# Layer 1: the shared expert's products moved into the router's block, its result kept and added among the routed experts

## The chip, the cores and the metric

The kernel runs on one core of one Trainium2 chip. The metric is the device time of one execution in microseconds; the time shown is the median of three runs. Beside it stands one profiled execution, from which all durations are read. Its span reaches from the first instruction to the last. The engines are TensorE (PE, with its weight loads as PEld), VectorE (DVE), ScalarE (ACT), GpSimd (POOL) and SyncE (SP), which issues the DMAs here.

## The reference, cut to what matters

The program is four layers of cross-attention and feed-forward network over 2048 tokens of 256 features. The change concerns the feed-forward network of layer 1 alone, a mixture of 32 experts with one shared expert:

```python
def _moe_forward(x3, gate_w, w_gate_up, w_down, ws_gate_up, ws_down):
    ...
    logits = x @ gate_w.T
    grouped = logits.reshape(T, G, E // G)                 # G = 8 groups of 4 experts
    group_scores = jnp.max(grouped, axis=-1)
    _, group_idx = jax.lax.top_k(group_scores, TG)         # TG = 3
    ...
    probs = jax.nn.softmax(scores.astype(jnp.float32), axis=-1)
    topk_w, topk_idx = jax.lax.top_k(probs, K)             # K = 6
    ...
    pos = jnp.take_along_axis(jnp.cumsum(oh, axis=0) - 1, flat_e[:, None], axis=1)[:, 0]
    valid = pos < C                                        # C = 48 places per expert
    ...
    out = jnp.einsum('tk,tkh->th', topk_w.astype(x.dtype), y_pairs)
    gu_s = x @ ws_gate_up
    gs, us = jnp.split(gu_s, 2, axis=-1)
    out = out + jax.nn.silu(gs) * us @ ws_down
    return out.reshape(b, s, h)

x = x + _L1_ffn_ref(_layernorm(x, axis=-1), ...)
```

It is applied to 16 blocks of 128 tokens, each with its own counting of places. The last three lines of the function are the shared expert. It needs the normalised rows and its weights, nothing of the router.

## The kernel before, in words

`stage_l1_experts` (line 2120) holds the tokens in `X`, 16 tiles of 128 tokens by 256 features in SBUF. It is a sequence of blocks. Within a block each engine has its own instruction list, written out by hand, and waits on semaphores; between blocks all engines meet at a barrier, and a `Stage` clears its semaphores in a small block of its own when it closes. No planner orders anything: the order of the code is the order of each queue.

The blocks of the layer are, in order:

- `f1n` (`normalised_transposed`, line 1121): statistics, normalised rows, their transposes into `xnt` (2 x 2048 columns). The loads of the shared expert's weights (`w13_raw`, `w2`) are issued there.
- `f1g` (`router_logits`, line 1169): 32 products on TensorE, one copy of the logits on VectorE.
- `f1r`, the router's block: VectorE finds the groups (`choose`, "cg"), masks, takes the softmax (exponential on ScalarE), chooses six experts ("ch"); TensorE counts (`earlier`, `sums`, lines 2230 and 2232); VectorE turns counts into places; TensorE transposes the places (line 2236), VectorE copies them (line 2222). SyncE issues the loads of the first six pairs of routed experts.
- `f1d`, the dispatch: one-hot rows on VectorE, products on TensorE (line 2311) bring the tokens to their experts.
- `f1w`, the routed experts: 16 rounds, a pair of experts each; VectorE multiplies (line 2433) and writes results (line 2437).
- `f1c`, the combine: products back to the tokens, added to `X` (lines 2500, 2502).
- `f1e`, the shared expert (`GatedExperts.run`): for each quarter of 512 tokens and each of three tiles of 128 hidden features, a gate and an up product (line 1340), Silu on ScalarE (line 1380), the multiplication on VectorE (line 1394) and the down product (line 1358); then the result is added to `X` (line 1400). To keep precision, rows and weights are split into a high part (rounded to fp32r) and a low part (the rest), and each product is three products: high by high, high by low, low by high. GpSimd splits the weights and three quarters of the rows there, ScalarE and VectorE the first quarter.

Then the statistics of layer 2's attention begin (`a2s`, line 128).

## Time and profile before

| what | value |
|---|---|
| median of three runs | 3017.01 us (3011.09, 3017.01, 3017.39) |
| profiled execution, its own time | 3011.44 us |
| its span | 3009.7 us |
| mean granted clock of TensorE | 0.889 |
| busy: PE, PEld, DVE, ACT, POOL | 77%, 56%, 62%, 49%, 51% |
| layer 1's feed-forward network, from statistics to next statistics | 684.4 to 1039.4 us |

### The profile page before, as it was taken

The page shows a single profiled execution, that of the slowest core. Times are in us where ns is not written, and L with a number is a line of the kernel's source. Part 1 is how long each engine was busy: PE and PEld are TensorE (multiplying, and loading weights), DVE is VectorE, ACT ScalarE, POOL GpSimd, SP SyncE. Part 2 cuts the span into 40 slices and gives each one's busy share as a digit, 9 for nine tenths or more (in the row PEclk, how much of TensorE's full clock was granted, in tenths as well). Part 3 has the DMA queues.
Part 4 walks back from the last instruction along what each step waited for, and adds up shares of the span by engine and source line. Part 5 has one row for each costly group of instructions (what it writes and reads, how often), then busy time and mean ns, then how long its engine had stood idle before and what let it go on. Part 6 is the DMA issues. An engine that isn't in the chain of part 4 may idle for free. (4 is left out here: it accounts for less than half of the span.)

```text
span 3009.7 us, 46369 instructions
## 1 busy us (share of the span) xinstructions
PE 2304.6 (77%) x14574; PEld 1687.5 (56%) x14574; DVE 1877.6 (62%) x3732; ACT 1484.4 (49%) x3339; POOL 1525.3 (51%) x1499
## 2 busy tenths in 40 slices
PE   4887133873888757669738888886999996899997
PEld 2333011433545634358527776764788885788885
DVE  3776486654536225445568888875688885666565
ACT  0667252660120025524348777775777874344443
POOL 5542002620000244148347777772888883688882
PEclk9999665895999869979869999998999998899999
DMA  5242101543040033323220000001000000244343
GB/s 128 61 96 62 42 0 33 147 138 118 4 173 1 23 78 81 81 74 101 65 85 1 0 0 0 0 15 65 6 5 5 3 2 18 74 112 113 101 117 90
DMA packets 119749, 174.62 MB, mean 58 GB/s; under 512 B 25389, under 2 KB 79693, under 8 KB 116383
## 3 DMA queue, kind: packets, MB, share of 16 engines
q1 hardware_dynamic: 119583, 172.53, 20.4%
q8 instruction: 90, 1.47, 0.2%
q14 instruction: 76, 0.62, 0.1%
HBM read 122.49 MB, written 11.48 MB: 45 GB/s over the span
## 5 line engine op out<-in xcount | busy, mean ns | idle before, releaser
L478 DVE TENSOR_REDUCE a_mraw<-a_first_ps 128x4 f32<-128x1024 f32 (+1 forms) x256 | 310.7, 1222 | 146.8 <-PE a_first_ps L329 146.5
L386 ACT ACTIVATE a_et<-a_second_ps 128x1024 f32<-128x1024 f32 x256 | 262.2, 1024 | 161.6 <-PE a_second_ps L347 159.6
L2804 POOL TENSOR_SCALAR a3x_raw<-a3x_raw,a3x_mu,a3x_dev 128x128 f32<-128x128 f32 x320 | 282.4, 895 | 5.2 <-issue 5.2
L2804 POOL TENSOR_SCALAR a3o_raw<-a3o_raw,a3o_mu,a3o_dev 128x128 f32<-128x128 f32 x256 | 231.7, 916 | 4.8 <-issue 4.8
L1712 DVE TENSOR_TENSOR f3e_hidden_low<-f3e_hidden,f3e_hidden_high 128x512 fp32r<-128x512 f32 x96 | 116.0, 1209 | 126.3 <-ACT f3e_hidden_high L1670 125.9
L1581 POOL TENSOR_TENSOR f3e_product<-f3e_silu,f3e_up 128x512 f32<-128x512 f32 x96 | 143.3, 1495 | 72.0 <-PE f3e_u_ps L1597 44.9
L364 PE MATMUL a_o_ps<-a_et,a_vt 128*32 128x256 f32 x2048 | 167.4, 399 | 7.4 <-ACT a_osb L416 6.1
L347 PE MATMUL a_second_ps<-a_qs,a_ks 64*128 64x256 bf16 (+2 forms) x896 | 117.7, 298 | 64.7 <-ACT a_et L386 54.7
L329 PE MATMUL a_first_ps<-a_ks,a_qs 64*128 64x256 bf16 (+2 forms) x1280 | 122.4, 266 | 18.9 <-DMA a_ks<-a_parts 10.2
L347 PEld LDWEIGHTS a_second_ps<-a_qs,a_ks 64*128 64x128 bf16 (+1 forms) x896 | 42.0, 96 | 165.3 <-ACT a_et L386 129.2
L1706 DVE TENSOR_TENSOR f3e_hidden<-f3e_product,f3e_spread 128x512 f32<-128x512 f32 x96 | 125.1, 1304 | 6.8 <-DMA f3e_spread<-f3e_shares 6.8
L1663 ACT ACTIVATE f3e_silu<-f3e_g_ps 128x512 f32<-128x512 f32 x96 | 57.5, 599 | 144.2 <-PE f3e_g_ps L1597 137.2
L2974 ACT ACTIVATE a3x_weights<-a3x_s_ps,a3x_nmax 128x128 f32<-128x128 f32 x256 | 91.1, 377 | 59.6 <-DVE a3x_nmax L3108 59.6
L2795 POOL TENSOR_TENSOR a3o_dev<-a3o_var,a3o_minus_half 128x24 f32<-128x24 f32 x16 | 69.0, 4309 | 96.9 <-DVE a3o_var L3096 96.9
L1322 POOL CAST f_w_high<-f_w_raw 128x512 fp32r<-128x512 f32 x3 | 2.8, 942 | 219.9 <-SPq L1301 219.9
L2974 ACT ACTIVATE a3o_weights<-a3o_s_ps,a3o_nmax 128x128 f32<-128x128 f32 x256 | 93.0, 410 | 26.9 <-DVE a3o_nmax L3108 26.4
L2933 PE MATMUL a3o_o_ps<-a3o_wparts,a3o_catq 128*128 128x256 bf16 x768 | 102.5, 287 | 0.8 <-DVE a3o_catq L3128 0.7
L2852 PE MATMUL a3o_p_ps<-a_wq,a3o_xq 128*128 128x512 f32 x256 | 81.7, 446 | 27.2 <-ACT a3o_vv L2989 16.5
L2852 PE MATMUL a3x_p_ps<-a_wkv,a3x_ctx_parts 128*128 128x512 f32 x384 | 101.7, 408 | 0.0
L2795 POOL TENSOR_TENSOR a3x_dev<-a3x_var,a3x_minus_half 128x24 f32<-128x24 f32 x16 | 69.0, 4311 | 59.8 <-DVE a3x_var L3096 59.8
L329 PEld LDWEIGHTS a_first_ps<-a_ks,a_qs 64*128 64x128 bf16 (+1 forms) x1280 | 71.6, 100 | 45.5 <-issue 16.4
L2933 PE MATMUL a3x_o_ps<-a3x_wparts,a3x_catq 128*128 128x256 bf16 x768 | 94.2, 273 | 0.7 <-DVE a3x_catq L3128 0.7
(547 smaller groups left out, 6968.3 us busy)
## 6 DMA issues: line engine op xcount, KB each, us to landing
f_w<-in_f_w SPq DMA_DIRECT2D x16, 1216.0 KB, 8.5
a_qs<-a_parts SPq DMA_DIRECT2D x144, 128.0 KB, 2.4
f_raw<-in_f_w SPq DMA_DIRECT2D x60, 256.0 KB, 3.4
a_ks<-a_parts SPq DMA_DIRECT2D x96, 128.0 KB, 2.4
f3e_spread<-f3e_shares SPq DMA_DIRECT2D x64, 192.0 KB, 3.0
f2e_spread<-f2e_shares SPq DMA_DIRECT2D x36, 256.0 KB, 3.4
f3e_spread<-f3e_shares SPq DMA_DIRECT2D x64, 128.0 KB, 3.1
f_raw<-in_f_w SPq DMA_DIRECT2D x60, 128.0 KB, 3.4
```

What stands on the lines that cost most here:

```text
L329: last = nc.tensor.matmul(self.first_ps[:, g % 2, u, c * N:c * N + N], self.queries(p, self.ROWS, b, tq, rows), self.keys(p, self.ROWS, b, ...
L347: last = nc.tensor.matmul(out, self.keys(p, self.ROWS_WITH_MAXIMA, b, t, rows), self.queries(p, self.ROWS_WITH_MAXIMA, b, tq, slice(0, N)) ...
L364: last = nc.tensor.matmul(self.o_ps[32 * j:32 * j + 32, columns], self.vt[:, b // 2 % self.NV, b % 2, c, self.block(k, j), :], self.et[:, ...
L386: self.nc.scalar.activation(self.et[:, g % self.WAVES_HELD, :, :], self.second_ps[:, :, :], ACT.Exp, scale=self.scale).then_inc(self.e_rea ...
L478: v.tensor_reduce(out, self.first_ps[:, g % 2, :, :].rearrange("p u (c n) -> p u c n", n=N), AX.X, ALU.max).then_inc(self.max_taken, 1)
L1581: nc.gpsimd.tensor_tensor(product[:, n % self.PRODUCTS, :], silu[:, n % 2, :], up[:, n % 2, :], ALU.mult).then_inc(product_ready, 1)
L1706: nc.vector.tensor_tensor(hidden[:, n % 3, :], product[:, n % self.PRODUCTS, :], spread[:, n % self.SPREAD, :], ALU.mult).then_inc(hidden_ ...
L2795: nc.gpsimd.tensor_tensor(dev[:, :], var[:, :], minus_half[:, :], ALU.pow)
L2804: mm = nc.gpsimd.tensor_scalar(head, head, mu[:, h:h + 1], dev[:, h:h + 1], ALU.subtract, ALU.mult)
L2852: mm = nc.tensor.matmul(out, lhs, rhs, start=(i == 0), stop=(i == len(pairs) - 1))
L2933: mm = nc.tensor.matmul(o_ps[:, 0:D], catq[:, u % 2, h, :], wparts[:, p, 4 * u + h, :], start=(u == 0 and h == 0 and p == 0), stop=(u == U ...
L2974: mm = nc.scalar.activation(weights[:, u % 2, h, :], s_ps[:, h, :], ACT.Exp, bias=nmax[:, u % 2, h:h + 1], accum_out=total[:, u % 2, h:h + 1])
```

## The change

The shared expert's block `f1e` at the end is gone. Its work is spread over three earlier places:

- In the logits' block, ScalarE rounds all rows and weights to their high parts and VectorE subtracts to get the low parts, beside the logits' products on TensorE.
- In the router's block, TensorE has the twelve gate-and-up pairs and four quarters of the down product in its list, and the router's count and transposes stand between them at fixed places. VectorE's twelve hidden products stand between the router's steps, given by the argument `between` of `choose` and `softmax_rows`. ScalarE has the Silus around the exponential, and copies the result of each quarter to a tile `shared_y`. The intermediate tiles lie in the room of `xnt`. The counts, and the transposes after them, share two banks of PSUM, so that the transposes now come in four parts.
- In the routed experts, VectorE adds one tile of `shared_y` to `X` behind each of the 16 results.

```diff
-def router_logits(nc, xnt, gate, n_experts, logits, name):
-
...
-def choose(nc, values, k, n, chosen, st, name):
+def choose(nc, values, k, n, chosen, st, name, between=lambda place: None):
...
         v.max(top[:, b, :], values[:, b, :])
+    between("maxima")
...
+        if step == 4:
+            between("counts")
...
+    between("ranks")
...
+        between(dve)
...
-class GatedExperts:
...
+    def logits_and_parts(self, xnt, gate, n_experts, logits, name):
...
                 @block.scalar
                 def _(act):
-                    nc.scalar.copy(self.x_high[:, 0, :, :], xnt[:, :, rows(0)]).then_inc(x_high_ready, 1)
                     for tb in range(4):
-                        for t in range(L):
-                            n = tb * L + t
-                            act.wait_ge(gate_done, n + 1)
-                            wait(act, hidden_ready, n - 1)
-                            nc.scalar.activation(silu[:, n % 2, :], g_ps[:, n % 2, :], ACT.Silu).then_inc(silu_ready, 1)
+                        rows = slice(tb * 512, tb * 512 + 512)
+                        nc.scalar.copy(self.x_high[:, :, rows], xnt[:, :, rows]).then_inc(x_split, 1)
+                    act.wait_ge(self.w_in, 16 * len(self.loads))
+                    nc.scalar.copy(self.high[:, :, :, :, :], self.raw[:, :, :, :, :]).then_inc(w_high, 1)
 
                 @block.vector
                 def _(dve):
-                    dve.wait_ge(x_high_ready, 1)
-                    nc.vector.tensor_tensor(self.x_low[:, 0, :, :], xnt[:, :, rows(0)],
-                                            self.x_high[:, 0, :, :].bitcast(F32), ALU.subtract
-                                            ).then_inc(x_low_ready, 1)
                     for tb in range(4):
-                        for t in range(L):
-                            n = tb * L + t
-                            dve.wait_ge(silu_ready, n + 1)
-                            dve.wait_ge(up_done, n + 1)
-                            wait(dve, down_done, n - 1)
-                            last = nc.vector.tensor_tensor(hidden[:, n % 2, :], silu[:, n % 2, :], u_ps[:, n % 2, :],
-                                                           ALU.mult)
-                            last.then_inc(hidden_ready, 1)
-                        dve.wait_ge(down_done, tb * L + L)
-                        for k in range(4):
-                            x = X[:, tb * 4 + k, :]
-                            last = nc.vector.tensor_tensor(x, x, y_ps[:, k, 0:D], ALU.add)
-                        last.then_inc(added, 1)
+                        rows = slice(tb * 512, tb * 512 + 512)
+                        dve.wait_ge(x_split, tb + 1)
+                        nc.vector.tensor_tensor(self.x_low[:, :, rows], xnt[:, :, rows],
+                                                self.x_high[:, :, rows].bitcast(F32), ALU.subtract)
+                    dve.wait_ge(w_high, 1)
+                    nc.vector.tensor_tensor(self.low[:, :, :, :, :], self.raw[:, :, :, :, :],
+                                            self.high[:, :, :, :, :].bitcast(F32), ALU.subtract)
+                    dve.wait_ge(logits_done, 1)
+                    nc.vector.tensor_copy(logits[:, :, :], lp[:, :, :])
...
+    def pe_gate_up(self, pe, n):
+        tb, t = divmod(n, self.TILES)
+        wait(pe, self.silu_ready, n - 1)
+        self.product(self.g_ps[:, n % 2, :], t, 0, tb).then_inc(self.gate_done, 1)
+        wait(pe, self.hidden_ready, n - 1)
+        self.product(self.u_ps[:, n % 2, :], t, 1, tb).then_inc(self.up_done, 1)
+
+    def pe_down(self, pe, tb):
+        L = self.TILES
+        pe.wait_ge(self.hidden_ready, tb * L + L)
+        wait(pe, self.y_kept, tb)
+        for k in range(4):
+            for t in range(L):
+                last = self.nc.tensor.matmul(self.y_ps[:, k, :], self.hidden[:, tb % 2, t, k * P:k * P + P],
+                                             self.w2[:, t, :], start=(t == 0), stop=(t == L - 1))
+        last.then_inc(self.down_done, 1)
+
+    def act_silu(self, act, n):
+        act.wait_ge(self.gate_done, n + 1)
+        wait(act, self.hidden_ready, n - 1)
+        self.nc.scalar.activation(self.silu[:, n % 2, :], self.g_ps[:, n % 2, :], ACT.Silu).then_inc(self.silu_ready, 1)
+
+    def act_keep(self, act, tb):
+        act.wait_ge(self.down_done, tb + 1)
+        for h in range(2):
+            k = 2 * h
+            last = self.nc.scalar.copy(self.y[:, 4 * tb + k:4 * tb + k + 2, :], self.y_ps[:, k:k + 2, :])
+        last.then_inc(self.y_kept, 1)
+
+    def dve_hidden(self, dve, n):
+        tb, t = divmod(n, self.TILES)
+        dve.wait_ge(self.silu_ready, n + 1)
+        dve.wait_ge(self.up_done, n + 1)
+        wait(dve, self.down_done, tb - 1)
+        self.nc.vector.tensor_tensor(self.hidden[:, tb % 2, t, :], self.silu[:, n % 2, :], self.u_ps[:, n % 2, :],
+                                     ALU.mult).then_inc(self.hidden_ready, 1)
...
+                        for n in range(3):
+                            shared.act_silu(act, n)
+                        on_act(act)
+                        for n in range(3, 6):
+                            shared.act_silu(act, n)
+                        shared.act_keep(act, 0)
+                        shared.act_silu(act, 6)
+                        shared.act_silu(act, 7)
+                        shared.act_keep(act, 1)
+                        for n in range(8, 11):
+                            shared.act_silu(act, n)
+                        shared.act_keep(act, 2)
+                        shared.act_silu(act, 11)
+                        shared.act_keep(act, 3)
+
+                        def between_groups(place):
+                            if place == "ranks":
+                                shared.dve_hidden(dve, 0)
+
+                        def between_experts(place):
+                            shared.dve_hidden(dve, {"maxima": 3, "counts": 4, "ranks": 5}[place])
+
+                        def take_turned(k):
+                            dve.wait_ge(turned_done, k + 1)
+                            v.tensor_copy(placet[0:E, k * 512:k * 512 + 512], counts[0:E, k % 2, :]).then_inc(turned_taken, 1)
+
+                        choose(nc, group_top, KG, G, keep, rt, "cg", between_groups)
+
+                        v.tensor_tensor(grouped, grouped, keep[:, :, :].unsqueeze(3).broadcast_to([P, B, G, E // G]),
+                                        ALU.mult)
+                        shared.dve_hidden(dve, 1)
+                        v.drain()
+                        on_dve(dve)
+                        choose(nc, logits, K, E, chosen, rt, "ch", between_experts)
+                        v.tensor_copy(valid[:, :, :], chosen[:, :, :]).then_inc(chosen_ready, 1)
+
+                        shared.dve_hidden(dve, 6)
+                        dve.wait_ge(counted, 1)
...
+                        shared.dve_hidden(dve, 7)
+                        v.tensor_tensor(place1[:, :, :], src[:, :, :], earlier[:, :, :], ALU.add)
...
+                        take_turned(0)
+                        take_turned(1)
+                        shared.dve_hidden(dve, 8)
+                        take_turned(2)
+                        take_turned(3)
+                        for n in range(9, 12):
+                            shared.dve_hidden(dve, n)
+
...
+                        def turn(k):
+                            pe.wait_ge(places_ready, 1)
+                            wait(pe, turned_taken, k - 1)
+                            for b in range(4 * k, 4 * k + 4):
+                                last = nc.tensor.transpose(counts[0:E, k % 2, (b % 4) * P:(b % 4) * P + P],
+                                                           place1[:, b, :], ident[:, :])
+                            last.then_inc(turned_done, 1)
+
+                        for n in range(6):
+                            shared.pe_gate_up(pe, n)
+                        shared.pe_down(pe, 0)
+                        shared.pe_gate_up(pe, 6)
+                        count()
+                        shared.pe_gate_up(pe, 7)
+                        shared.pe_down(pe, 1)
+                        turn(0)
+                        turn(1)
+                        shared.pe_gate_up(pe, 8)
+                        turn(2)
+                        turn(3)
+                        shared.pe_gate_up(pe, 9)
+                        shared.pe_gate_up(pe, 10)
+                        shared.pe_down(pe, 2)
+                        shared.pe_gate_up(pe, 11)
+                        shared.pe_down(pe, 3)
...
                                                                ALU.mult, ALU.subtract).then_inc(y_taken, 1)
+                                x = X[:, q - 2, :]
+                                nc.vector.tensor_tensor(x, x, shared_y[:, q - 2, :], ALU.add)
...
-        experts.run(X, xnt, "f1e")
```

On TensorE in the router's block, before (names: `f1r_earlier` and `f1r_sums` are the two counts, `f1r_turned` the transposes):

```order
L1175 UNCONDITIONAL_BRANCH
L2224 UNCONDITIONAL_BRANCH [waits barrier_Pool_Activation_PE_DVE_SP_release]
L2230 MATMUL f1r_earlier<-f1r_chosen,f1r_before 128x512 [waits f1r_chosen_ready,f1r_const_in]
L2232 MATMUL f1r_sums<-f1r_chosen,f1r_ones 128x512
L2236 MATMUL f1r_turned<-f_ident,f_place 32x128 [waits f1r_places_ready]
L2236 MATMUL f1r_turned<-f_ident,f_place 32x128 x15
L2167 UNCONDITIONAL_BRANCH
```

Now, the piece of the same block around the count (`f1r_g_ps` and `f1r_u_ps` are gate and up, `f1r_y_ps` down, `f1r_counts` the counts); this is the first quarter of down, pair 6 and the count:

```order
L1336 MATMUL f1r_y_ps<-f1h_w,f1h_xnt 128x256 [waits f1r_hidden_ready]
L1336 MATMUL f1r_y_ps<-f1h_w,f1h_xnt 128x256 x11
L1319 MATMUL f1r_g_ps<-f1h_x_high,f1h_w_high 128x512 [waits f1r_silu_ready]
L1319 MATMUL f1r_g_ps<-f1h_x_high,f1h_w_high 128x512
L1319 MATMUL f1r_g_ps<-f1h_x_low,f1h_w_high 128x512 x2
L1319 MATMUL f1r_g_ps<-f1h_x_high,f1h_w_low 128x512 x2
L1319 MATMUL f1r_u_ps<-f1h_x_high,f1h_w_high 128x512 [waits f1r_hidden_ready]
L1319 MATMUL f1r_u_ps<-f1h_x_high,f1h_w_high 128x512
L1319 MATMUL f1r_u_ps<-f1h_x_low,f1h_w_high 128x512 x2
L1319 MATMUL f1r_u_ps<-f1h_x_high,f1h_w_low 128x512 x2
L2225 MATMUL f1r_counts<-f1r_chosen,f1r_before 128x512 [waits f1r_chosen_ready,f1r_const_in]
L2226 MATMUL f1r_counts<-f1r_chosen,f1r_ones 128x512
```

The count stands behind seven gate-and-up pairs and one quarter of down in TensorE's queue, where it was first in its block.

On VectorE in the router's block, before, at the end of the groups' choice (`f1r_keep` marks the groups kept):

```order
L1217 COPY f1r_cg_run<-f1r_cg_run 128x16x4
L1220 TENSOR_TENSOR f1r_keep<-f1r_cg_run,f1r_cg_count 128x128
L1222 SCALAR_TENSOR_TENSOR f1r_keep<-f1r_keep,f1r_cg_equal 128x128
L1224 TENSOR_TENSOR f1r_keep<-f1r_keep,f1r_cg_above 128x128
L2193 TENSOR_TENSOR f1r_logits<-f1r_logits,f1r_keep 128x512
L1241 TENSOR_REDUCE f1r_sm_max<-f1r_logits 128x16
L1243 TENSOR_TENSOR f1r_probs<-f1r_logits,f1r_sm_max 128x512
```

Now (the rows that write `f1h_xnt` are hidden products of the shared expert, in the room of `xnt`):

```order
L1196 COPY f1r_cg_run<-f1r_cg_run 128x16x4
L1357 TENSOR_TENSOR f1h_xnt<-f1h_xnt,f1r_u_ps 128x512 [waits f1r_up_done,f1r_silu_ready]
L1202 TENSOR_TENSOR f1r_keep<-f1r_cg_run,f1r_cg_count 128x128
L1204 SCALAR_TENSOR_TENSOR f1r_keep<-f1r_keep,f1r_cg_equal 128x128
L1206 TENSOR_TENSOR f1r_keep<-f1r_keep,f1r_cg_above 128x128
L2180 TENSOR_TENSOR f1r_logits<-f1r_logits,f1r_keep 128x512
L1357 TENSOR_TENSOR f1h_xnt<-f1h_xnt,f1r_u_ps 128x512 [waits f1r_up_done,f1r_silu_ready]
L1223 TENSOR_REDUCE f1r_sm_max<-f1r_logits 128x16
L1225 TENSOR_TENSOR f1r_probs<-f1r_logits,f1r_sm_max 128x512
L1357 TENSOR_TENSOR f1h_xnt<-f1h_xnt,f1r_u_ps 128x512 [waits f1r_up_done,f1r_silu_ready]
```

Three hidden products stand in this piece, each with a wait for a Silu and an up product, and the router's steps are queued behind them.

On TensorE behind the combine, before (line 2476 is the combine's last product, line 1340 the shared expert's):

```order
L2476 MATMUL f1c_out_ps<-f1x_results,f1c_back 128x512 x8
L2454 UNCONDITIONAL_BRANCH
L1332 UNCONDITIONAL_BRANCH
L1340 MATMUL f1e_g_ps<-f_x_high,f_w_high 128x512 x2
L1340 MATMUL f1e_g_ps<-f_x_low,f_w_high 128x512 x2
L1340 MATMUL f1e_g_ps<-f_x_high,f_w_low 128x512 x2
L1340 MATMUL f1e_u_ps<-f_x_high,f_w_high 128x512 x2
L1340 MATMUL f1e_u_ps<-f_x_low,f_w_high 128x512 x2
```

Now (line 2493 is the same last product, line 1032 belongs to layer 2's attention):

```order
L2493 MATMUL f1c_out_ps<-f1x_results,f1c_back 128x512 x8
L2471 UNCONDITIONAL_BRANCH
L1006 UNCONDITIONAL_BRANCH
L1032 MATMUL a_m_ps<-a_ident,a_xn 128x128 x4
L1040 MATMUL a_m_ps<-a_xt,a_wq 128x256 x4
L1049 MATMUL a_m_ps<-a_ctx,a_wk 64x256 x2
```

The shared expert's products no longer stand between the combine and the next layer.

## Rows read from the trace of the kernel before

**Rows 1.** Windows: stretch us, busy us (instructions) per engine, granted clock, DMA
```profile
976.20:1039.40 63.20, 55.35 (x240) 46.37 (x240) 15.90 (x31) 8.23 (x13) 16.83 (x13) 0.94 0.00 1
717.96:754.30 36.34, 6.78 (x20) 3.39 (x20) 26.13 (x83) 0.63 (x1) 1.80 (x1) 0.58 0.52 209
```

**Rows 2.** Timeline, ends of the shared expert: start, us, engine, line, work [idle<-releaser]
```profile
975.79 0.42 DVE L2502 TENSOR_TENSOR X<-X,f1c_out_ps 128x256 f32<-128x256 f32 x1
...
977.02 1.04 ACT L1374 CAST f_x_high<-f_xnt 128x1024 fp32r<-128x1024 f32 x1 [104.98 <-PEq L43]
...
1035.55 1.42 DVE L1400 TENSOR_TENSOR X<-X,f1e_y_ps 128x256 f32<-128x256 f32 x4 [2.71 <-PE f1e_y_ps L1358]
...
1039.39 5.32 DVE L128 BATCH_NORM_STATS2 a2s_stats<-X  x16 [2.43 <-SPq L43]
```

**Rows 3.** Timeline, TensorE's weight loads in the shared expert
```profile
980.12 0.50 PEld L1340 LDWEIGHTS f1e_g_ps<-f_x_high,f_w_high 128*128 128x128 f32 x2 [7.77 <-issue]
...
984.39 0.41 PEld L1340 LDWEIGHTS f1e_g_ps<-f_x_high,f_w_high 128*128 128x128 f32 x2
...
987.11 1.71 PEld L1358 LDWEIGHTS f1e_y_ps<-f_w,f1e_hidden 128*128 128x128 f32 x8
...
988.84 0.41 PEld L1340 LDWEIGHTS f1e_g_ps<-f_x_high,f_w_high 128*128 128x128 f32 x2
```

**Rows 4.** Timeline, VectorE in the router's block
```profile
718.00 0.69 DVE L2189 TENSOR_REDUCE f1r_group_top<-f1r_logits 128x128 f32<-128x512 f32 x1 [0.64 <-PEq L43]
...
722.06 0.29 DVE L1220 TENSOR_TENSOR f1r_keep<-f1r_cg_run,f1r_cg_count 128x128 f32<-128x128 f32 x1
...
737.80 0.43 DVE L2198 COPY f1r_valid<-f1r_chosen 128x512 f32<-128x512 f32 x1
...
741.86 0.09 DVE L2201 MEMSET f1r_totals<- 128x32 f32 x1 [3.63 <-PE f1r_sums L2232]
...
752.02 2.28 DVE L2222 CAST f_placet<-f1r_turned 32x2048 bf16<-32x2048 f32 x1 [3.54 <-PE f1r_turned L2236]
```

**Rows 5.** Windows over the logits' products and the shared expert's start
```profile
703.20:717.40 14.20, 13.38 (x64) 13.28 (x64) 0.69 (x1) 0.00 (x0) 0.00 (x0) 0.52 0.00 1
...
984.00:988.00 4.00, 4.00 (x20) 3.33 (x19) 1.08 (x2) 0.60 (x1) 3.18 (x2) 1.00 0.02 4
```

**Rows 6.** Groups by line: names, shapes, count | busy us, mean ns | idle
```profile
L1394 DVE TENSOR_TENSOR f1e_hidden<-f1e_silu,f1e_u_ps 128x512 f32<-128x512 f32 x12 | 8.3, 688 | 32.1 <-PE f1e_u_ps L1340 28.0 <-ACT f1e_silu L1380 4.1
...
L1380 ACT ACTIVATE f1e_silu<-f1e_g_ps 128x512 f32<-128x512 f32 x12 | 7.2, 599 | 46.1 <-PE f1e_g_ps L1340 46.1
...
L1400 DVE TENSOR_TENSOR X<-X,f1e_y_ps 128x256 f32<-128x256 f32 x16 | 5.7, 417 | 10.8 <-PE f1e_y_ps L1358 10.8
...
L1385 DVE TENSOR_TENSOR f_x_low<-f_xnt,f_x_high 128x1024 fp32r<-128x1024 f32 x1 | 2.0, 1957 | 1.9 <-ACT f_x_high L1374 1.9
```

**Rows 7.** Group by line: a fp32r subtraction of 128x1024 on VectorE
```profile
L2566 DVE TENSOR_TENSOR a_wkv<-a_wraw,a_wkv 128x1024 fp32r<-128x1024 f32 x4 | 4.9, 1224 | 4.5 <-ACT a_wkv L2558 4.5
```

**Rows 8.** Timeline, ScalarE: a copy, and a table load with its neighbours
```profile
663.86 0.58 ACT L416 COPY a_osb<-a_o_ps 128x512 f32<-128x512 f32 x1
...
1116.11 1.28 ACT L386 ACT_TABLE_LOAD   x1
1117.41 1.02 ACT L386 ACTIVATE a_et<-a_second_ps 128x1024 f32<-128x1024 f32 x1
```

**Rows 9.** Timeline, VectorE in two rounds of the routed experts
```profile
835.18 0.34 DVE L2433 TENSOR_TENSOR f1w_gated<-f1w_silu,f1w_gu_ps 128x176 f32<-128x176 f32 x1 [0.54 <-ACT f1w_silu L2416]
...
837.73 0.34 DVE L2433 TENSOR_TENSOR f1w_gated<-f1w_silu,f1w_gu_ps 128x176 f32<-128x176 f32 x1 [0.54 <-ACT f1w_silu L2416]
```

**Rows 10.** Timeline, TensorE in the first rounds of the dispatch
```profile
760.61 5.14 PE L2311 MATMUL f1d_x_ps<-f1d_hot,f1d_parts 128*128 128x512 f32 x12 [8.70 <-DVE f1d_parts L2290]
...
766.46 3.03 PE L2311 MATMUL f1d_x_ps<-f1d_hot,f1d_parts 128*128 128x512 f32 x12
```

325 lines of the change are left out of this document (123 added, 202 removed).

## The prediction, made before the changed kernel ran

> **What bounds the kernel now.** I read the windows by stage first. The shared expert of layer 1 stands alone at the end of that layer: from 976.2 to 1039.4 TensorE is busy 55.35 of 63.20 us at a granted clock of 0.94, and VectorE only 15.90 [rows 1]. The router's block, 717.96 to 754.30, is the mirror image: VectorE 26.13 of 36.34 us, TensorE 6.78, granted clock 0.58 [rows 1]. So one stretch is bound by TensorE, the other by a chain of small VectorE steps, and nothing of the first needs anything of the second: both read only the transposed rows. The timeline shows how far the shared expert is exposed: VectorE ends the routed part at 975.79 + 0.42 = 976.21 and starts the next layer's statistics at 1039.39 [rows 2]. Everything between is on the path.
>
> **Term 1, what goes: -61.2 us.** Of the 63.18 us between 976.21 and 1039.39, two stage boundaries (drain, semaphore clears, new block) take 977.02 - 976.21 = 0.81 and 1039.39 - (1035.55 + 1.42) = 2.42 [rows 2]. Afterwards there is one. It cannot cost less than the smaller nor more than the larger; I take 2.0, nearer the second, because the layer's stage still closes there, less the clears of the shared expert. 63.2 - 2.0 = 61.2, with bounds 60.8 and 62.4.
>
> **Term 2, the router's block grows: +24.4 us.** I price TensorE's new programme from starts of its weight loads in the shared expert. The first gate-and-up pair (12 products of 512 columns) takes 984.39 - 980.12 = 4.27 us from cold, the next 987.11 - 984.39 = 2.72, eight passes of the down product 988.84 - 987.11 = 1.73 [rows 3]. A quarter of the down product is 24 passes, 5.19. The counting products held VectorE 3.63 us and the transposes 3.54 at the low level [rows 4]: half is 1.7 each. Sum: 4.27 + 11 x 2.72 + 4 x 5.19 + 1.7 + 1.7 = 58.4.
>
> Then the waits, by a schedule from the block's start, t = 0 at 718.00 [rows 4]. Each hidden product adds 0.69 to VectorE, each Silu takes 0.60 on ScalarE [rows 6]. TensorE's pairs end at 4.3, 7.0, 9.7, 12.4, 15.2 and 17.9, the first quarter of down at 23.1, pair 6 at 25.8; then comes the count. VectorE reaches the place of the first hidden product at 722.06 - 718.00 = 4.06 and waits about half a microsecond for the up product's end and the semaphore; the second and third wait as little. Before, it had the experts chosen at 737.80 + 0.43 - 718.00 = 20.2 [rows 4]; with six hidden products and 1.4 of waits it is 20.2 + 4.1 + 1.4 = 25.7. So both come to the count at about the same time, and TensorE is the later by nothing to speak of. The count ends at 27.5. From there the places took 752.02 - 3.54 - 741.86 = 6.6 [rows 4]; with one more hidden product VectorE has them near 35.0, while TensorE, with pair 7 and the second quarter of down, comes to the transposes at 35.4. Neither wait decides, by 0.1 and 0.4 us. From there VectorE only follows. In total it has 36.3 less its two waits, 29.1, plus 12 x 0.69 = 37.4 of 58.4. One wait of TensorE remains: after the last up product it has nothing in front of the last down, and stands for 0.69 and two semaphore steps, 0.9. Behind the last product ScalarE keeps two 128x512 tiles, 0.58 each [rows 8], and the step to it is 0.2: 1.4. Total 58.4 + 0.9 + 1.4 = 60.7, against 754.30 - 718.00 = 36.3 before: +24.4. If TensorE were warm from the start it would be 1.6 less (4.27 against 2.72).
>
> ScalarE changes its table three times in the block. A load takes 1.28 us: it starts at 1116.11, right behind the copy ahead of it, and the operation behind it at 1117.41 [rows 8]. The first hides before the first gate product, the third behind the exponential. The second stands between the third Silu, done near 9.3, and the exponential, which ends near 11.2; VectorE is done with the third hidden product at 10.7 and waits about as long as it waited for the exponential before. So nothing is added. The Trainium skill (ScalarE: Activation LUTs, What ACT_TABLE_LOAD costs) adds a drain of about 1.38 us to every switch. The trace disagrees: no such gap stands on either side of that load. With the page's figure the exponential and the count come 1.4 us later and the sum is about 1.3 higher.
>
> **Term 3, parts beside the logits: 0.** In the logits block ScalarE now rounds the rows (four of 1.04) and the weights (128x1536), VectorE subtracts. VectorE's 128x1024 subtraction is 1.96 us where GpSimd works beside it [rows 6], and 1.22 for the same shape elsewhere [rows 7]. GpSimd is idle here. With the rounding of the first rows at 1.04 [rows 2], VectorE is done even by the dear end at 703.2 + 1.1 + 4 x 1.96 + 1.5 x 1.96 = 715.1; the logits come at 716.7, after 13.38 us of products [rows 5]. By the cheap end it is done by 711. Cover 1.6 us or more; if it went, each microsecond would count. The loads of these weights were issued there before as well.
>
> **Term 4, the adds among the routed experts: +0.35 us.** Sixteen adds of 128x256 go behind the sixteen result steps on VectorE. The nearest row is the add of the same shape with one operand in PSUM, 0.42 [rows 6]. In a round VectorE stands idle 0.54 us right there, waiting for the next Silu [rows 9], so the add fits with 0.1 to 0.2 to spare. Only the last one, behind the last result, is exposed: 0.35. Bounds: 0 and 16 x 0.42 = 6.7, if the gap were not where the row has it. I take 0.35 since gap and add are both rows.
>
> **Term 5, closing the block: +0.4.** Nine more semaphores are cleared in the two stages (seven and two). The larger boundary costs 1.61 more than the smaller for 18 more of them, at most 0.09 each; I take half, since it closes a stage more; bounds 0 and 0.8 [rows 2].
>
> **What stays.** Before, TensorE starts the dispatch from cold: 12 products in 5.14 us, later 3.03 [rows 10]. Now it works until 1.4 us before the block's end, but the wait for the places and the first rows stays about 6 us, so it stands some 7.5; and 7.77 us of idleness before the shared expert, which came out of a busy stretch, ended in a cold start [rows 3]. I book nothing; bounds -2.1 and 0.
>
> Sum: -61.2 + 24.4 + 0 + 0.35 + 0.4 = -36.0. The profiled execution spans 3009.7 us and took 3011.4; so span 2973.7 and time 2975.4. The median of the three timed runs is 5.6 above the profiled one (3011.1, 3017.0, 3017.4 in all), so taken from the median it is 2981. I forecast 2979, between the two and nearer the median.
>
> **Rivals.**
> A, the clock stays at 1.2 GHz in the router's block; this is my rival on the slower side. For it: the logits kept TensorE busy 13.38 of 14.20 us and the granted clock stood at 0.52 [rows 5], so being busy is not enough there. Against it: these same products of 512 columns were granted 1.00 from 984 on [rows 5], 4 us after starting, in the same ping-pong with ScalarE and VectorE. The work of 58.4 - 1.6 = 56.8 at the high level doubles at the low one to 113.6, the block becomes 115.9 with its wait and tail, +79.6, and the span 3009.7 - 61.2 + 79.6 + 0.75 = 3028.9: time 3031, slower by 0.6%. Each microsecond of that work done at the low level costs one more; the gain is used up when some 37 of the 56.8 run low, and it is measurably slower from 43. Hence a part of A (a clock that swings, a quarter of the work low) gives 2975.4 + 14 = 2990. The Trainium skill (TensorE: Matmul & The Clock Gate, A second HAM failure mode: psum-queue depth-cycling) says that short idle gaps between groups of products that cycle through PSUM banks can make the clock swing between its levels. By that rule with half the work low the time would be 3004. The shared expert cycles through two banks for each of its outputs and shows 1.00, so the trace disagrees so far.
>
> B, the two programmes do not mesh: VectorE comes late to the count and to the places, TensorE stands, and each stall shifts everything behind it. For it: margins of 0.1 and 0.4 us, and twelve fixed places for hidden products. Against it: VectorE's work is 37 of 61 us, and a lag of 1 us at either place costs 1. I allow 1 to 5 in all: time 2976 to 2980, with the median's offset 2982 to 2986.
>
> C, the adds are on the path in the routed experts: up to 6.7, time 2982, with the median's offset 2987. For it: a gap with 0.1 us to spare. Against it: a round there is 837.73 - 835.18 = 2.55 us [rows 9].
>
> D, the change doesn't do what it says: some barrier or shared tile puts the expert behind the router again, the block is 36.3 + 60 and the time as before. Against it: TensorE's order has seven pairs ahead of the count, and they wait for nothing of the router.
>
> **How the numbers follow.** Forecast with its own range 2972 to 2987: 0.83. B beyond 2 us 0.07, C 0.04, A in part (swinging) 0.03, A whole 0.01, D 0.02. The range 2970 to 2989 takes in B, C and the offset between profile and median; some 0.1 is left outside, most of it above. A measurement of this kernel tells some 0.2%, 6 us. Faster by more 0.96, within 0.03, slower 0.01.
>
> **What would show it.** The profile after should have: no stretch of TensorE alone between the combine and the next layer, 2 us there; the router's block 60 to 62 us long with granted clock over 0.9 after its first 4 us; the logits' copy right behind the last logit product; VectorE's wait for the count under 2 us in place of 3.63; rounds of the routed experts still 2.55 us. It is wrong if TensorE's idle time in the block is over 3 us, if the granted clock there is under 0.85, or if the rounds grow by 0.1 us or more.

## The result, and the profile after

| | before | after |
|---|---|---|
| median of four timed runs of the same job | 3014.66 us (3011.09 to 3017.39) | 2970.82 us (2969.27 to 2980.76) |
| profiled execution, its own time | 3011.44 us | 2972.09 us |
| its span | 3009.7 us | 2970.3 us |
| mean granted clock | 0.889 | 0.895 |
| layer 1's network, from its statistics to the next ones | 684.42 to 1039.39: 354.97 us | 687.57 to 1003.98: 316.41 us |

The ratio is 0.9865, 95% interval 0.9847 to 0.9883: the kernel is 1.35% faster. The forecast was 2979.0 us with a range of 2970 to 2989; the median lies 8 us under the forecast and inside the range, by 0.8 us: the lower end was 2970.

Layer 1 divides into these stretches, read from the timelines: the first product is TensorE's, all other starts and ends are VectorE's or ScalarE's (the combine's start is its first `f1c_back`):

| stretch | before | after | difference |
|---|---|---|---|
| statistics to the first logits product | 18.84 | 18.47 | -0.37 |
| logits' products to the logits' copy | 13.41 | 11.34 | -2.07 |
| logits' copy to the router's first step | 1.33 | 1.39 | +0.06 |
| router's block to its last result | 36.30 | 61.20 | +24.90 |
| boundary to the dispatch | 3.84 | 4.14 | +0.30 |
| dispatch and routed experts | 114.41 | 114.69 | +0.28 |
| to the combine's first step | 5.30 | 6.43 | +1.13 |
| combine | 98.36 | 96.93 | -1.43 |
| combine's end to the next statistics | 63.18 | 1.82 | -61.36 |
| sum | 354.97 | 316.41 | -38.56 |

Outside these stretches the two profiles have 2654.7 and 2653.9 us: the layer's statistics start 3.15 us later after the change, and from the next statistics to the end it is 4.0 us less.

The windows after, in the columns of [rows 1] (a stretch, its length, busy time of TensorE, its weight loads, VectorE, ScalarE and GpSimd, granted clock, DMA). The first is the router's block, the other two split it at 723 us:

```profile
718.76:779.98 61.22, 59.26 (x260) 48.51 (x260) 34.11 (x98) 15.95 (x24) 1.78 (x1) 0.97 0.31 125
718.76:723.00 4.24, 4.23 (x11) 3.38 (x12) 3.62 (x26) 1.85 (x2) 1.78 (x1) 0.56 0.63 203
723.00:779.98 56.98, 55.03 (x251) 45.13 (x249) 30.49 (x72) 14.10 (x22) 0.00 (x0) 1.00 0.28 119
```

The block that had TensorE at 6.78 of 36.34 us [rows 1] has it at 59.26 of 61.22, and the clock stands at 1.00 from the second pair to the end.

VectorE in that block and at the end of the layer (timeline; the bracket is the idle time before an instruction and what ended it), to be read against [rows 2, 4]:

```profile
723.60 0.69 DVE L1357 TENSOR_TENSOR f1h_xnt<-f1h_xnt,f1r_u_ps 128x512 f32<-128x512 f32 x1 [0.84 <-PE f1r_u_ps L1319]
...
726.34 0.69 DVE L1357 TENSOR_TENSOR f1h_xnt<-f1h_xnt,f1r_u_ps 128x512 f32<-128x512 f32 x1 [0.35 <-PE f1r_u_ps L1319]
...
730.21 0.69 DVE L1228 TENSOR_REDUCE f1r_sm_total<-f1r_probs 128x16 f32<-128x512 f32 x1 [0.46 <-ACT f1r_probs L1220]
...
746.82 0.09 DVE L2190 MEMSET f1r_totals<- 128x32 f32 x1 [1.01 <-PE f1r_counts L2226]
...
755.23 1.28 DVE L2173 CAST f_placet<-f1r_counts 32x512 bf16<-32x512 f32 x2 [1.10 <-PE f1r_counts L2232]
...
1001.74 0.42 DVE L2519 TENSOR_TENSOR X<-X,f1c_out_ps 128x256 f32<-128x256 f32 x1
1003.98 2.38 DVE L128 BATCH_NORM_STATS2 a2s_stats<-X  x7 [1.81 <-PEq L43]
```

VectorE's waits for the count and the transposes, 3.63 and 3.54 before [rows 4], are 1.01 and 1.10. The tail of 63.18 us is one boundary of 1.82.

TensorE around the count and the transposes, and at the block's end (timeline):

```profile
744.41 0.62 PE L1319 MATMUL f1r_u_ps<-f1h_x_high,f1h_w_low 128*128 128x512 f32 x2
744.86 1.02 PE L2225 MATMUL f1r_counts<-f1r_chosen,f1r_before 128*128 128x512 f32 x2
745.72 1.02 PE L2226 MATMUL f1r_counts<-f1r_chosen,f1r_ones 128*128 128x512 f32 x2
746.18 1.03 PE L1319 MATMUL f1r_g_ps<-f1h_x_high,f1h_w_high 128*128 128x512 f32 x2
...
749.35 5.34 PE L1336 MATMUL f1r_y_ps<-f1h_w,f1h_xnt 128*128 128x256 f32 x24
754.53 1.04 PE L2232 MATMUL f1r_counts<-f_ident,f_place 128*32 128x128 f32 x8
755.32 0.70 PE L1319 MATMUL f1r_g_ps<-f1h_x_high,f1h_w_high 128*128 128x512 f32 x2
...
773.42 5.45 PE L1336 MATMUL f1r_y_ps<-f1h_w,f1h_xnt 128*128 128x256 f32 x24 [0.84 <-DVE f1h_xnt L1357]
```

Neither the count nor the transposes carry a bracket: TensorE came to both without idling, and stood only once, 0.84 us ahead of the last quarter of down.

### The profile page after: what moved, and what is told of

Same layout as the page of the kernel before. It is cut to its first block and busy times, and to the rows that moved or that the text cites. A ratio compares the mean times of both kernels' runs of the same rounds, so it can differ in the third digit from the quotient of the medians.

```text
span 2970.3 us, 46347 instructions
## 1 busy us (share of the span) xinstructions
PE 2299.3 (77%) x14574; PEld 1684.4 (57%) x14574; DVE 1884.8 (63%) x3739; ACT 1496.7 (50%) x3353; POOL 1513.7 (51%) x1487
## 5 line engine op out<-in xcount | busy, mean ns | idle before, releaser
L329 PE MATMUL a_first_ps<-a_ks,a_qs 64*128 64x256 bf16 (+2 forms) x1280 | 122.8, 267 | 20.6 <-DMA a_ks<-a_parts 10.4
```

Of the source, the lines that this page charges most:

```text
L329: last = nc.tensor.matmul(self.first_ps[:, g % 2, u, c * N:c * N + N], self.queries(p, self.ROWS, b, tq, rows), self.keys(p, self.ROWS, b, ...
```

## The experiments

A stretch that no edit touches varies from profile to profile, so two numbers are given for each: the time, and the stretch from the logits' copy to the next layer's statistics, which holds the edits' effects but leaves out the logits' products. It is 322.72 us before and 286.60 after. The ratio compares a kernel with the kernel before in the same job, a set of runs on one chip; the medians of before in the five jobs were 3014.66 (first), 3012.43 (repeated, without the additions, count late, warm dispatch), 3012.07 (separate blocks, parts alone), 3010.12 (early constants, early and warm, one block) and 3012.40 (last). So times of different jobs differ by 2 us or more without an edit.

| kernel | median of its runs | ratio to before, interval | logits' products | copy to next statistics |
|---|---|---|---|---|
| before (profile) | | | 13.38 | 322.72 |
| changed kernel, first job | 2970.82 | 0.9865 (0.9847, 0.9883) | 11.30 | 286.60 |
| repeated | 2972.60 | 0.9867 (0.9850, 0.9883) | 11.47 | 286.31 |
| repeated, last job | 2971.36 | 0.9861 (0.9846, 0.9876) | 13.09 | 286.31 |
| without the additions | 2972.79 | 0.9867 (0.9851, 0.9884) | 11.45 | 286.62 |
| count late | 2981.57 | 0.9893 (0.9877, 0.9910) | 13.11 | 296.38 |
| warm dispatch | 2970.32 | 0.9861 (0.9844, 0.9877) | 11.71 | 282.25 |
| separate blocks | 3008.74 | 0.9989 (0.9980, 0.9999) | 13.07 | 320.22 |
| parts alone | 3004.58 | 0.9977 (0.9966, 0.9987) | 12.94 | 320.98 |
| early constants | 2969.47 | 0.9868 (0.9852, 0.9884) | 13.27 | 282.46 |
| early and warm | 2967.63 | 0.9857 (0.9841, 0.9874) | 13.12 | 279.42 |
| early and warm, last job | 2966.44 | 0.9850 (0.9836, 0.9863) | 11.66 | 279.28 |
| early, warm, one block | 2968.44 | 0.9856 (0.9839, 0.9873) | 13.18 | 279.51 |

**The overlap alone.** All products of the shared expert in a block of their own ahead of the router's:

```diff
                 with nc.Block() as block:
...
+                    @block.vector
+                    def _(dve):
+                        for n in range(12):
+                            shared.dve_hidden(dve, n)
...
+                    @block.tensor
+                    def _(pe):
+                        for tb in range(4):
+                            shared.pe_gate_up(pe, 3 * tb)
+                            if tb:
+                                shared.pe_down(pe, tb - 1)
+                            shared.pe_gate_up(pe, 3 * tb + 1)
+                            shared.pe_gate_up(pe, 3 * tb + 2)
+                        shared.pe_down(pe, 3)
+                with nc.Block() as block:
+                    on_act, on_dve = softmax_rows(nc, block, logits, probs, E, rt, "sm")
...
-                        for n in range(6):
-                            shared.pe_gate_up(pe, n)
-                        shared.pe_down(pe, 0)
-                        shared.pe_gate_up(pe, 6)
                         count()
-                        shared.pe_gate_up(pe, 7)
-                        shared.pe_down(pe, 1)
                         turn(0)
```

> The changed kernel with all of the shared expert's products, Silus and hidden products in a block of their own ahead of the router's block, nothing interleaved; parts beside the logits and additions among the routed experts stay. My theory (the gain is the overlap of a block bound by TensorE with one bound by VectorE's chain): the separate block takes 58 to 60 us, the router's block is again 36 us, together about 96 against 61.2, so 34 to 36 us slower than the changed kernel, and 8 to 11 us faster than the kernel before. Rival (the gain comes from the closed stage, the parts made early and the result kept, and not from the overlap): within 10 us of the changed kernel.

Measured beside the repeated kernel: 3008.74 against 2972.60 in time (+36.1, with before at 3012.07 and 3012.43 in their two jobs), 320.22 against 286.31 in the stretch (+33.9; the copy to the dispatch is 98.77 against 66.58, +32.2, the rest +1.7). Windows over the two blocks, columns as above:

```profile
719.90:777.96 58.06, 55.55 (x240) 46.30 (x240) 8.26 (x13) 12.80 (x22) 0.04 (x1) 0.97 0.00 1
777.96:813.40 35.44, 7.14 (x20) 3.09 (x20) 26.50 (x86) 1.87 (x2) 1.76 (x1) 0.61 0.53 215
```

58.06 + 35.44 = 93.5 us one after the other against 61.2 beside each other. So 32 of the 36 us are the overlap. The expected 8 to 11 us under before was my slip: with 34 to 36 of a gain of 40 undone, 4 to 6 remain; measured are 3.3, and in the stretch 2.5. The rival, that moving and keeping are the gain, falls.

**The parts alone.** The kernel before, with rounding and subtractions beside the logits (`logits_and_parts` as in the change) and the shared expert still at the end:

```diff
-                        nc.gpsimd.tensor_copy(self.x_high[:, tb % 2, :, :], xnt[:, :, rows(tb)]).then_inc(x_next_high, 1)
...
-                    nc.scalar.copy(self.x_high[:, 0, :, :], xnt[:, :, rows(0)]).then_inc(x_high_ready, 1)
...
-            router_logits(nc, xnt, gate, E, logits, "f1g")
+            experts.logits_and_parts(xnt, gate, E, logits, "f1g")
```

> The kernel before with one part of the change alone: the rows and weights of the shared expert are rounded and split beside the logits' products; the shared expert still stands at the end of the layer. My theory (the parts hide behind the logits, and at the end of the layer they delay only the first products): the logits' block ends as before within 0.5 us, the shared expert's 62.4 us fall to 58 to 60, the time is 2 to 4 us under that of the kernel before. Rival 1: the parts beside the logits delay the logits' copy, which comes later than 4 us after the last part, and the gain is gone. Rival 2: the parts were the bound of the shared expert, and it falls by more than 6 us.

The tail, from the combine's end to the next statistics, is 60.20 us against 63.18, -2.98, and the first gate product shows where from (timeline, TensorE; VectorE's last addition ends at 978.86 + 0.42 = 979.28):

```profile
980.11 1.19 PE L1349 MATMUL f1e_g_ps<-f_x_high,f_w_high 128*128 128x512 f32 x2 [4.26 <-PEq L43]
```

It starts 0.83 us after the last addition; before it was 980.12 - 976.21 = 3.91 [rows 2, 3]. VectorE ends the parts at 712.87 and waits 5.63 us for the logits, so Rival 1 falls. Rival 2 falls too: the shared expert's part fell by 3 us and not by over 6. The time is 7.5 us under before, where 2 to 4 were expected; the stretch has only 322.72 - 320.98 = 1.7 of it, and I can name no stage for the rest (more under the account of the prediction).

**The place of the count.**

```diff
                         shared.pe_gate_up(pe, 6)
-                        count()
                         shared.pe_gate_up(pe, 7)
                         shared.pe_down(pe, 1)
+                        count()
                         turn(0)
```

> The changed kernel with the count moved in TensorE's list behind the eighth gate-and-up pair and the second quarter of the down product, directly ahead of the transposes. My theory (the count's place matters since the work behind it covers VectorE's 6.6 us from count to places): VectorE waits about 8 us instead of 1.01 for the count, TensorE stands 6 to 7 us before the transposes, the router's block grows from 61.2 to 67 to 68 us, the time rises by 6 to 7 us. Rival (the order within the block is of no account, since TensorE has work enough): the block stays within 1 us of 61.2.

The rival falls: router's start to dispatch is 74.86 us against 65.18, +9.7, and the time +9.0. That is 3 us more than I expected. TensorE at the transposes (timeline):

```profile
755.72 1.02 PE L2225 MATMUL f1r_counts<-f1r_chosen,f1r_before 128*128 128x512 f32 x2
756.58 1.02 PE L2226 MATMUL f1r_counts<-f1r_chosen,f1r_ones 128*128 128x512 f32 x2
765.05 1.89 PE L2232 MATMUL f1r_counts<-f_ident,f_place 128*32 128x128 f32 x8 [7.46 <-DVE f_weight L2207]
766.59 1.20 PE L1319 MATMUL f1r_g_ps<-f1h_x_high,f1h_w_high 128*128 128x512 f32 x2
767.59 1.05 PE L1319 MATMUL f1r_g_ps<-f1h_x_low,f1h_w_high 128*128 128x512 f32 x2
...
770.83 1.04 PE L2232 MATMUL f1r_counts<-f_ident,f_place 128*32 128x128 f32 x8
```

7.46 us are the idle wait. Behind it comes a cold start, that is, TensorE's first work at the lower level: the granted clock was 1.00 from 755.7 to 758, 0.50 from 765 to 768 and 1.00 again from 771. Eight transposes take 766.59 - 765.05 = 1.54 from start to start instead of 755.32 - 754.53 = 0.79, the pair after them 770.83 - 766.59 = 4.24 instead of 758.17 - 755.32 = 2.85. 7.46 + 0.75 + 1.39 = 9.6. So this stall cost itself and a cold start. Not every stall does: behind the 0.84 us ahead of the changed kernel's last quarter of down the granted clock stayed at 1.00, and the quarter took 5.45 us where others took 5.34.

**The additions among the routed experts.** This kernel leaves the shared expert's result out of the output.

```diff
-                                x = X[:, q - 2, :]
-                                nc.vector.tensor_tensor(x, x, shared_y[:, q - 2, :], ALU.add)
```

> The changed kernel without the sixteen additions of the shared result to the tokens among the routed experts; the shared expert is computed but its result is not added. My theory (the additions lie in VectorE's wait for the next Silu): the rounds of the routed experts keep their 2.55 us, dispatch to last result gets 0.3 to 0.5 us shorter, the time falls by under 1 us, which is not measurable. Rival C (they are on the path): the rounds get up to 0.42 us shorter and the time falls by up to 6.7 us.

Dispatch start to the combine's first addition: 142.05 us against 142.35, 142.49 and 142.31 in the three profiles of the changed kernel. By itself this difference of 0.3 to 0.4 says little, since that stretch is 141.78 before and 142.92 with the parts alone, on the same code without additions. The end of the last round shows it better (timeline, VectorE):

```profile
897.98 0.48 DVE L2452 SCALAR_TENSOR_TENSOR f1x_results<-f1w_y_ps,f1x_slot_weight,f1x_results 128x256 fp32r<-128x256 f32 x1
898.38 0.42 DVE L2457 TENSOR_TENSOR X<-X,f_shared_y 128x256 f32<-128x256 f32 x1
```

The last addition ends 898.80 - 898.46 = 0.34 us behind the last result. The time is the same (2972.79 and 2972.60). Two rounds with the additions (timeline, VectorE):

```profile
870.14 0.48 DVE L2452 SCALAR_TENSOR_TENSOR f1x_results<-f1w_y_ps,f1x_slot_weight,f1x_results 128x256 fp32r<-128x256 f32 x1 [1.18 <-ACT f1x_results L2439]
870.54 0.42 DVE L2457 TENSOR_TENSOR X<-X,f_shared_y 128x256 f32<-128x256 f32 x1
871.16 0.34 DVE L2448 TENSOR_TENSOR f1w_gated<-f1w_silu,f1w_gu_ps 128x176 f32<-128x176 f32 x1 [0.21 <-ACT f1w_silu L2431]
...
873.71 0.34 DVE L2448 TENSOR_TENSOR f1w_gated<-f1w_silu,f1w_gu_ps 128x176 f32<-128x176 f32 x1 [0.21 <-ACT f1w_silu L2431]
```

and one without them:

```profile
870.56 0.48 DVE L2452 SCALAR_TENSOR_TENSOR f1x_results<-f1w_y_ps,f1x_slot_weight,f1x_results 128x256 fp32r<-128x256 f32 x1 [1.19 <-ACT f1x_results L2439]
871.59 0.34 DVE L2448 TENSOR_TENSOR f1w_gated<-f1w_silu,f1w_gu_ps 128x176 f32<-128x176 f32 x1 [0.54 <-ACT f1w_silu L2431]
```

With the additions the wait for the Silu is 0.21 instead of 0.54, and the round is 2.55 us (873.71 - 871.16), as before [rows 9]. Rival C falls.

**The changed kernel once more,** twice, in two jobs, without an edit.

> The changed kernel once more, unchanged. It shows what a second profile differs by without an edit. My theory: the 2.0 us that the logits' products took less and the 4.0 us that the last layers took less than before vary from execution to execution with the granted clock, so each stage of layer 1 agrees within 0.3 us with the first profile, except those two, which may differ by 1 to 4 us. Rival (the change causes them): the logits' products again take 11.4 us and not 13.4, and the last layers again take 870.3 us and not 874.3.

> The changed kernel, unchanged, as the measure for the kernel timed beside it. Both theories: 2970 to 2973 us; the stretch from the logits' copy to the next layer again takes 286 to 287 us. The logits' products take either about 11.4 or about 13.2 us; by the theory that this is chance, either may come.

The stretch from the copy agrees within 0.3 us with the first profile (286.60, 286.31, 286.31). The logits' products took 11.30 and 11.47 us, which would speak for the rival, but 13.09 in the second repeat, on the same code; over the twelve profiles with the parts beside the logits, five took 11.3 to 11.7 us and the other seven 12.9 to 13.3. So that difference needs no cause in the change. The 0.37 us ahead of the products goes with it: statistics to first product is 18.1 to 18.5 us in those five profiles and 18.8 to 19.2 in the others, before included.

Of the last layers: from the next statistics to the end the three profiles show 1966.3, 1966.3 and 1966.1 us, the one of before 1970.3, so this time the rival's number came again; but the kernels whose code is the same there range from 1962.9 (count late) to 1972.9 (one block), and before lies inside. What lies ahead of the layer moved the other way: its statistics start at 684.42 before and at 687.57, 688.09 and 686.09 in the three (685.1 to 688.3 in all twelve). All that lies outside the layer is 2654.7 us before, 2653.9, 2654.4 and 2652.2 in the three, and 2651.2 to 2660.6 over the twelve. One profile of before can't tell whether its 1970.3 are its own.

**The cold start of the dispatch.**

```diff
+WARM = 6
...
+                        for k in range(WARM):
+                            nc.tensor.matmul(slot_ps[:, :], ident[:, :], place1[:, :, :].rearrange("p b e -> p (b e)"),
+                                             start=True, stop=True)
                         for b in range(B):
                             pe.wait_ge(hot_ready, b + 1)
```

> The changed kernel with six additional f32 products of 128x512 on TensorE at the start of the dispatch, whose result nothing reads; they run while TensorE would wait for the first rows. Theory 1 (what the dispatch loses at its start is the lower clock after a pause): the first twelve products take about 3.0 us instead of 4.95, the span falls by about 2 us. Rival (the pause is too long for them, or the first products wait for something else): the first twelve products still take about 5 us and the time is the same within 0.5 us. In the second case the six products themselves may cost 1 to 2 us if the first row comes before they end.

TensorE at the dispatch's start (timeline), the changed kernel:

```profile
786.58 4.95 PE L2326 MATMUL f1d_x_ps<-f1d_hot,f1d_parts 128*128 128x512 f32 x12 [7.71 <-DVE f1d_parts L2305]
```

and with the six products:

```profile
780.49 5.39 PE L2322 MATMUL f1d_slot_ps<-f_place,f_ident 128*128 128x512 f32 x12 [2.50 <-PEq L43]
785.86 3.06 PE L2330 MATMUL f1d_x_ps<-f1d_hot,f1d_parts 128*128 128x512 f32 x12
```

Theory 1 holds at this place: 3.06 instead of 4.95, and the first product comes 2.47 us after VectorE's start in both, so the additional ones delay nothing. The stretch fell by more, 4.1 us: the first two gate-and-up products of the routed experts, behind a pause of 1.45 us, took 2.59 us here and 4.28 in the changed kernel. That second 1.7 came in this profile alone: in the other eleven, and before, they took 3.9 to 4.3, with the early constants and four additional products 4.13 and 4.03. The time, 2970.32 against 2972.60, doesn't resolve it.

**A version that is faster.** The dispatch starts when `f1d_same` lands, the combine when `f1c_place` does, both issued only after their boundary. In the changed kernel (timeline):

```profile
781.70 0.43 SPq L2285 DMA_DIRECT2D f1d_same<-in_f_same  x1
784.11 0.41 DVE L2298 TENSOR_SCALAR f1d_xs<-X,f_mean,f_rstd 128x256 f32<-128x256 f32 x1 [10.74 <-DMA f1d_same<-in_f_same]
...
904.51 1.03 PE L2484 MATMUL f1c_pos_ps<-f_placet,f1c_owner 128*128 128x512 bf16 x2 [7.08 <-DMA f1c_place<-in_f_place]
```

So the constants are loaded one block ahead:

```diff
                             sp.dma_start(w[:, q, :, :], source[:, q, :, :]).then_inc(w_in[q], 16)
+                        sp.dma_start(places[:, :], dram["f1_places"]).then_inc(places_in, 16)
+                        sp.dma_start(same[:, :], dram["f1_same"]).then_inc(places_in, 16)
...
-                        sp.dma_start(places[:, :], dram["f1_places"]).then_inc(places_in, 16)
-                        sp.dma_start(same[:, :], dram["f1_same"]).then_inc(places_in, 16)
+                        sp.dma_start(owner[:, :, :].bitcast(I16), dram["f1_owner"]).then_inc(const_in, 16)
+                        sp.dma_start(place[:, :], dram["f1_place"]).then_inc(const_in, 16)
```

> The changed kernel with four small constant tensors loaded one block ahead of their use: those of the dispatch in the router's block, behind the loads of the routed experts' weights, those of the combine in the dispatch's block. My theory (behind the router's block and ahead of the combine the path is a DMA that is issued only after the boundary): 4.14 us between the router's block and the dispatch become 2.0 to 2.5, 6.43 us ahead of the combine's first step become 3 to 4, the time falls by 4 to 6 us, two of which may come back or go with the clock at the next start. Rival (the drain, the clears and the new block are the path there, and the DMA only ends last by a little): the time falls by under 1 us.

> The kernel with the early constants, and four additional f32 products of 128x512 at the start of the dispatch whose result nothing reads. My theory (the shorter pause of TensorE, some 5.5 us, still ends in the lower clock, and products that fill it avoid this): the dispatch's first twelve products take about 3.0 us instead of 4.9, the time is 2 us under that of the early constants alone. Rival (with the pause 2 us shorter the clock is already held): no difference beyond 0.5 us.

> The kernel with early constants and four additional products once more, timed beside the changed kernel on one chip. My theory (the stages from the logits' copy to the next layer are 7 us shorter, as its first profile has it: 279.4 against 286.6 and 286.3): the time is 5 to 8 us under that of the changed kernel of the same job. Rival (the later layers give the gain back): within 2 us of it.

The early constants shorten the stretch by 3.9 us (282.46 against 286.31). The two boundaries shrank by more than was expected, from 4.18 and 6.94 us in the repeat to 1.40 and 1.49, together 8.2; but 2.2 came back in the dispatch and the routed experts (116.83 against 114.63), 2.0 in the combine (98.37 against 96.35), for which I looked for no cause, and 0.3 at its end. In the time the early constants alone don't show: 2969.47 us is 0.9868 of before in that job, and the changed kernel has 0.9865, 0.9867 and 0.9861.

With four additional products the dispatch's first twelve took 3.06 us instead of 5.35, so the rival (the clock is already held) falls; the stretch is 279.42 and 279.28, and the time in the first of these jobs is 1.8 us under that of the early constants, which four runs each don't resolve. Timed in one job beside the changed kernel, early and warm took 2963.57 to 2968.46 us in five runs, the changed kernel 2968.84 to 2972.49 in four: medians 2966.44 and 2971.36, 4.9 us or 0.17% apart, with no run of the one in the range of the other; their intervals to before still overlap a little (0.9836 to 0.9863 and 0.9846 to 0.9876). All runs of the other jobs fit this too: 2966.01 to 2968.40 with early and warm, none of the changed kernel under 2968.84. The stretch has 7.0; some 2 us of it don't arrive in the medians. A part was given back right behind the boundary ahead of the dispatch. VectorE and GpSimd there (timeline of the last one):

```profile
780.09 1.80 POOL L2295 MEMSET f1d_wp<- 128x2048 f32 x1 [60.41 <-POOLq L43]
...
780.13 1.90 DVE L2304 TENSOR_SCALAR f1d_xs<-X,f_mean,f_rstd 128x256 f32<-128x256 f32 x1 [8.01 <-PEq L43]
```

VectorE's first step takes 1.90 us where it took 0.41 (1.90 or 1.91 in all four kernels with early constants), beside a memset of GpSimd that was over before this step while it waited for the DMA (781.33 + 1.80 = 783.13 against 784.11 in the changed kernel).

**One block for logits and router.**

```diff
-                shared.logits_and_parts(xnt, gate, E, logits, "f1g")
...
+                        shared.act_parts(act, xnt)
                         for n in range(3):
                             shared.act_silu(act, n)
...
+                        shared.dve_parts(dve, xnt, earlier, logits)
                         grouped = logits[:, :, :].rearrange("p b (g k) -> p b g k", g=G)
...
+                        shared.pe_logits(pe, xnt, gate, earlier)
                         for n in range(6):
                             shared.pe_gate_up(pe, n)
```

> The kernel with the early constants and the additional products, and the logits' block and the router's block made into one, the logits first in TensorE's list and the shared expert's pairs right behind them. My theory (one boundary goes, the first pair starts at the higher or the lower clock as the logits leave it): the distance from the logits' copy to the router's first step falls from 1.39 us to under 0.3, TensorE starts its first pair 1 us earlier or more, the time falls by 1 to 2 us more. Rival (TensorE's first pair then waits for VectorE's last subtraction, and nothing is gained): the same within 0.5 us.

From the copy's start to the router's first step it is 0.78 us instead of 1.39, where under 0.3 was expected; so 0.6 is gained there, and TensorE goes on to the first pair without a gap (logits from 706.67 for 13.18 us, the pair at 719.66). The block from there to the dispatch stays (62.32 against 62.38). The time, 2968.44 with runs from 2963.14 to 2974.09 against 2967.63 without this edit, doesn't show the expected 1 to 2, and with this spread it can't exclude them.

## Why the prediction was right

**Term 1** (-61.2): measured -61.36. One boundary of 1.82 instead of the 2.0 that I took.

**Term 2** (+24.4): measured +24.9, the block 61.2 against 60.7. Its sizes held: the first pair took 723.33 - 718.77 = 4.56 (4.27 forecast), the next 2.74 (2.72), and the eleven behind the first 31.2 together (29.9), since a pair takes longer behind the count (3.17) and behind a quarter of down (2.92); the four quarters of down 20.6 (20.8), the last stall 0.84 (0.9), the keeping 1.07 behind it (1.4 with its step). The count took 746.18 - 744.86 = 1.32 (1.7), the two halves of the transposes 0.79 each, 1.6 (1.7). So errors of up to 1.3 us cancelled in part, and 0.5 is left. The two narrow margins held: the choice ended at 744.08 + 0.43 = 744.51, 0.35 us ahead of the count (0.1 forecast), the places were ready at 753.45 + 0.68 = 754.13, 0.40 ahead of the transposes (0.4), and TensorE idled at neither. The first three hidden products waited 0.84, 0.35 and 0.49 us. That these margins carry weight is shown by the late count. The second table load hid as forecast: ScalarE's Silu ended at 728.23, and

```profile
728.25 1.28 ACT L1220 ACT_TABLE_LOAD   x1
729.54 0.63 ACT L1220 ACTIVATE f1r_probs<-f1r_probs 128x512 f32<-128x512 f32 x1
730.19 1.28 ACT L1343 ACT_TABLE_LOAD   x1
731.49 0.60 ACT L1343 ACTIVATE f1h_xnt<-f1r_g_ps 128x512 f32<-128x512 f32 x1
```

has no gap on either side of a load. The Trainium skill (ScalarE: Activation LUTs, What ACT_TABLE_LOAD costs) adds a drain of about 1.38 us to a switch; these rows disagree again, and VectorE waited 0.46 us for the exponential.

**Rival A** (the clock stays low): the granted clock was 1.00 over 56.98 of the 61.2 us, with the products cycling through two banks for each output. Against the rule of the Trainium skill that I had weighed (TensorE: Matmul & The Clock Gate, A second HAM failure mode: psum-queue depth-cycling), no swing shows here. But that rule asks for short idle gaps, and TensorE was busy 55.03 of these 56.98 us and idled once, 0.84 us, so the block hardly tests it. **Rival B** (no mesh): TensorE waited at neither the count nor the transposes; the late count shows what it would have cost. **Rival D** falls with the separate blocks.

**Term 3** (0): the four subtractions took 4.63 us together, 1.16 each, at the cheap end; VectorE waited 3.98 us for the last logits product. **Term 4** (+0.35): the last addition stands 0.34 us behind the last result, and the rounds stay 2.55 us. **Term 5** (+0.4): the two semaphores more are cleared behind the logits, +0.06, the seven more behind the router's block, +0.30. **What stays** (0): the dispatch starts cold, 4.95 us for its first products against 5.14 [rows 10]. Not forecast are 1.13 us more ahead of the combine and 1.43 less in it. With the parts alone, on the code of before, the combine's first step comes 6.15 us behind the last result (5.30 before) and the combine takes 96.91 (98.36), so these two need no cause in the change; that they cancel is luck.

The sum was -36.0. In the stretch that holds these terms the three profiles show -36.1, -36.4 and -36.4. The time fell by more: 43.8, 39.8 and 41.0 us in three jobs. Between the two first profiles it fell by 39.4 us of span, 3.4 more than the sum. Of these, 2.4 are the logits' products and what stands ahead of them, whose shorter length came in five profiles of twelve, while the one profile of before has the longer; 0.8 lie outside the layer (4.0 less behind it, 3.15 more ahead of it), less than what kernels with the same code differ by there; the rest is in the terms. So that these came on top is in part luck. Whether the later layers are systematically shorter stays open, since before has one profile. The kernel with the parts alone was 7.5 us faster with 1.7 us less in its stretch, and I can't place that rest either.

The error of the forecast, 8.2 us, comes apart into three. I took the median of three runs of before, 3017.0, for typical and added 3.6 to what the sum gave (2975.4) for the offset between profile and median. The later runs speak against it: 40 runs of before, in four jobs, have medians of 3010.1 to 3012.4, beside 3011.4 of the profiled execution. The three runs were high by chance, and the 3.6 had no ground. The changed kernel's own median lies 1.3 us under its profiled time, and the rest, 3.3, is the surplus above. The mechanism was right and so were the terms of layer 1. The time is only 0.8 us inside the range and 1.2 us under the narrower one of 2972 to 2987 that had the chance of 0.83.
